# Products without a reader on TensorE's waits: a mixture-of-experts and windowed-attention kernel on one core

## The reference

```python
x = x + L0_ffn(L0_cond(x, cond_256, cond_64, ...))   # low-rank mixing, then 8 experts, the best 2 per token
x = x + L1_ffn(L1_cond(x, cond_256, ...))            # rotation by quaternions, then 2 layers

def L0_cond(x, spectral, rank, input_basis, mode_to_rank, output_basis):
    mtr = orthogonalize(mode_to_rank)                # Cholesky of a 64x64 Gram matrix, then its inverse
    proj = einsum('bsd,kd->bsk', x, input_basis) * spectral
    return (proj @ mtr * rank) @ output_basis

def layer(x):                                        # x: 8 x 512 x 256, heads of 64, windows of 128
    q, k, v = split(shift(x) @ wqkv); q, k = rotary(l2norm(q), l2norm(k))
    x = x + local_attention(q, k, v) @ wo
    h = layernorm(shift(x)) @ w1 + b1                # mean, variance, then gate and value halves
    a, g = split(h)
    return x + (a * gelu(g)) @ w2 + b2
```

## Time and profile before

| | us |
|---|---|
| median of 3 runs | 1883.55 (1882.44 to 1883.98) |
| the profiled execution | 1891.32 |
| its span, first to last instruction | 1889.6 |
| TensorE busy with products | 1724.4 (91%) |
| VectorE busy | 1081.8 (57%) |
| ScalarE busy | 915.0 (48%) |
| mean granted clock of TensorE | 0.96 of full speed |

### The profile page before, as it was taken

How to read it: one execution, slowest core, us unless ns; L and a number is a source line. 1 busy time by engine, 2 the same in 40 slices (tenths; PEclk the granted TensorE clock), 3 DMA queues, 4 the chain that set the end, 5 groups by cost and what they waited for, 6 DMA issues and landing times.

```text
span 1889.6 us, 28122 instructions
## 1 busy us (share of the span) xinstructions
PE 1724.4 (91%) x8535; PEld 1013.8 (54%) x8537; DVE 1081.8 (57%) x2991; ACT 915.0 (48%) x2195; POOL 170.8 (9%) x281
## 2 busy tenths in 40 slices
PE   5869997789999999999999999999999999999987
PEld 2547886455554555545555555455555555555555
DVE  7753332466575556565665665556656655565652
ACT  2203332355555646455646464556464646464741
POOL 5023331210020002000200020002000000000000
PEclk8759999789999999999999999999999999999998
DMA  8714442210010011000100110001001000000000
GB/s 238 275 33 120 121 120 78 70 34 12 1 34 1 1 34 34 23 13 1 35 1 1 34 34 23 13 1 35 1 1 34 12 23 1 1 1 1 1 23 11
DMA packets 59107, 72.31 MB, mean 38 GB/s; under 512 B 16644, under 2 KB 44888, under 8 KB 58840
## 3 DMA queue, kind: packets, MB, share of 16 engines
q1 hardware_dynamic: 50088, 58.77, 9.5%
q0 software_dynamic: 5376, 10.76, 2.3%
q10 hardware_dynamic: 3504, 1.06, 0.2%
HBM read 50.64 MB, written 19.92 MB: 37 GB/s over the span
## 4 chain that ended last, share of the span: by engine, by line
PE 68%; DVE 7%; issue 6%; ACT 1%; another core or an unknown queue 0%; DMA 0%; DVEq 0%; POOL 0%; ACTq 0%; POOLq 0%
PE pj L1444 16%; PE pj L1532 16%; PE pj L1538 7%; PE pj L1510 6%; PE sc L1467 6%; PE ob L1493 4%; PE pt L1478 3%; PE pj L1452 2%; PE pj L1434 1%; DVE pT L1346 1%; PE pj L1502 1%; DVE swapped L1721 1%; PE pj L1516 1%; PE pj L1544 1%; PE pj L1520 1%
## 5 line engine op out<-in xcount | busy, mean ns | idle before, releaser
L1444 PE MATMUL pj<-wqkv,xT 128*128 128x512 f32 x768 | 349.3, 605 | 6.4 <-issue 6.4
L1532 PE MATMUL pj<-xsq,w 128*128 128x512 f32 (+3 forms) x748 | 321.0, 579 | 6.5 <-DVE hid L1811 4.5
L1613 ACT ACTIVATE prob<-prob,nm 128x256 f32<-128x256 f32 (+1 forms) x512 | 239.8, 469 | 122.8 <-DVE nm L1750 118.0
L1750 DVE CUSTOM_DVE_ANT_0 prob<-sc,mask 128x256 f32<-128x256 f32 (+1 forms) x512 | 170.0, 386 | 132.4 <-issue 132.4
L1444 PEld LDWEIGHTS pj<-wqkv,xT 128*128 128x128 f32 x768 | 145.5, 193 | 184.7 <-issue 183.0
L1532 PEld LDWEIGHTS pj<-xsq,w 128*128 128x128 f32 (+1 forms) x748 | 137.3, 191 | 151.5 <-issue 145.3
L1716 DVE TENSOR_TENSOR direct<-qkraw,tabs 128x1024 f32<-128x1024 f32 x64 | 78.4, 1226 | 134.6 <-ACT qkraw L1584 134.6
L1478 PEld LDWEIGHTS pt<-ident,prob 128*128 128x128 f32 x896 | 105.0, 141 | 91.6 <-issue 65.3
L1478 PE MATMUL pt<-ident,prob 128*128 128x128 f32 x896 | 127.3, 276 | 23.8 <-DVE pT L1346 18.5
L1159 PE MATMUL yb<-w2m,hT 128*128 x576 | 136.3, 391 | 10.3 <-issue 8.5
L1467 PE MATMUL sc<-kT,qT 64*128 64x256 f32 (+1 forms) x1024 | 132.3, 377 | 14.1 <-DVE nm L1750 14.1
(11 more groups left out here) (306 smaller groups left out, 2254.9 us busy)
## 6 DMA issues: line engine op xcount, KB each, us to landing
w1x<-w_folded SPq DMA_DIRECT2D x72, 128.0 KB
slots_y<-yt SPq DMA_DIRECT2D x36, 256.0 KB
x1tok<-in_x_dram SPq DMA_DIRECT2D x10, 512.0 KB, 4.4
w1m<-in_L_ffn_w_dram SPq DMA_DIRECT2D x8, 512.0 KB, 5.6
w2m<-in_L_ffn_w_dram SPq DMA_DIRECT2D x8, 512.0 KB, 9.1
x_after_moe<-x1tok SPq DMA_DIRECT2D x8, 512.0 KB
x1out<-x_after_moe SPq DMA_DIRECT2D x8, 512.0 KB
out_dram<-x1out SPq DMA_DIRECT2D x7, 512.0 KB, 2.9
```

The lines of the kernel that those rows point to most:

```text
L1444: mm = pe.matmul(o[:, :], xs(s, c, w * P, P), wqkv[:, l, c, k * INNER:(k + 1) * INNER], start=(c == 0), stop=(c == DC - 1))
L1532: mm = pe.matmul(o[0:P if j == NJ - 1 else HJ[j], 0:tn], cols, h[:, c, t0:t1], start=(c == 0), stop=(c == DC - 1))
L1613: ins = a.activation(prob[:, g % 4, hh, 0:n], prob[:, g % 4, hh, 0:n], ACT.Exp, bias=nm[:, g % 4, hh:hh + 1], scale=-1.0, accum_out=rs[:, ...
L1750: ins = v.tensor_tensor_reduce(prob[:, g % 4, hh, 0:n], sc[par][:, hh, 0:n], mask[:, w % 2, 0:n], -1.0, 3.0e38, ALU.add, ALU.min, nm[:, g ...
```

## The change

TensorE gets further products whose results nobody reads. They are float32, 128x128 by 128x512, and each overwrites the same bank. In the routing there are 11 behind the router product, 1 behind L757, 6 behind L761 and 2 behind L764, each group ahead of the wait that follows. In the layers there are 12 behind the wait for `edge`, and in the second half of the last feed-forward 4 ahead of the wait of `mean`, 7 ahead of that of `var` and 7 ahead of that of the first `gate`. No wait, buffer or other instruction is changed.

```diff
                     router_product()
+                    def idle_products(count):
+                        for _ in range(count):
+                            pe.matmul(xb[:, 3, :], ident[:, :], projT_all, start=True, stop=True)
+                    projT_all = projT[:, 0, 0:512]
+                    idle_products(11)
                     pe.wait_ge(v_prep, AT_3)
                     pe.matmul(rk[lo, K + 3 * Q:K + 4 * Q], EHQ[hi, :], elim[hi, 1, :], start=True, stop=True
                               ).then_inc(quad_full, 1)
+                    idle_products(1)
                     pe.wait_ge(UT_copied, 1)
                     pe.wait_ge(w1p_copied, E)
                     pe.matmul(pb[0:K, 0:K], UT[:, :], rawT[:, :], start=True, stop=True).then_inc(mtr_full, 1)
+                    idle_products(6)
                     pe.wait_ge(z_ready, 1)
                     ...
                     mm.then_inc(m_full, 1)
+                    idle_products(2)
                     pe.wait_ge(m_ready, 1)
...
+                    def idle_products(count):
+                        for _ in range(count):
+                            pe.matmul(ob[:, :, :].rearrange("p c r -> p (c r)"), ident[:, :], rot[:, :, :].rearrange("p c d -> p (c d)"),
+                                      start=True, stop=True)
                     pe.wait_ge(edge, 1)
+                    idle_products(12)
...
                         elif kind == "mean":
+                            if t0 > 0:
+                                idle_products(4)
                             pe.wait_ge(xsum_ready, at(st["ffn"], i, FFN, 1, 1))
                             ...
                         elif kind == "var":
+                            if t0 > 0:
+                                idle_products(7)
                             pe.wait_ge(var_in, at(st["ffn"], i, FFN, 1, 1))
                             ...
                         elif kind in ("gate", "value"):
                             j = st["j"]
+                            if t0 > 0 and kind == "gate" and j == 0:
+                                idle_products(7)
                             pe.wait_ge(h_ready, at(st["ffn"], i, FFN, DC, DC))
```

## The result

The changed kernel takes **1908.24 us** (median of 4 runs, 1901.69 to 1910.95) against 1883.19 for the kernel before beside it: a ratio of 1.0125, 95% interval 1.0104 to 1.0146, so 20 to 27 us slower. The forecast was 1899, range 1891 to 1909: the sign is right, the time lies at the range's upper end, and some 9 us were not foreseen.

What follows compares the result with a forecast made beforehand. TensorE's chain (68% of the span) was taken as the bound, with waits and half clock behind them. Routing +7.3, lead +1, last half feed-forward +6.9 sum to +15.2 on 1883.55: 1899 us, range 1891 to 1909.

Steps and rivals of the forecast that it cites:

- The price of a product: All three places: a float32 product is two records, 0.86 us at 2.4 GHz and 1.71 us at 1.2 GHz.
- the bound of 3.6: TensorE's clock: from dense work to full clock takes 5 us, with 3.6 and 6 as bounds.
- The routing's terms: Routing, 20 products: the groups' overruns less the time given back by the clock, +7.3 us, bounds +6.0 and +11.4.
- from M's start to the hot products: Routing: the 64 records of L774 take 3.5 to 4 us at full clock instead of about 7.1, giving back 3.1.
- the second rival: Routing: its delay is hidden if the experts start on something other than the index; 7.3 falls away, 1891.5 us; 6%.
- The tail's terms: Last half feed-forward: +2.2, +3.7, +3.3 in the waits, -3.05 at the gates, +0.8 behind; sum +6.9 us.
- the term of the Gelu wait: Tail, behind the gates: the clock may fall in the wait for Gelu, +1.6 us at most, taken as +0.8.
- The lead's size: Lead, 12 products: +1 us taken, between -3.3 and +6.5, with +2.9 at the end of the first QKV.
- ScalarE's unexplained wait: Lead: a remote wait of 3.85 us until 350.70; ending as before, it swallows the 2.9 us delay.
- the sum's last: Whole kernel: +15.2 us from the profiled execution carried over unchanged to the median, 1883.55 + 15.2 = 1898.8 us.
- The first rival: All three places: a product takes one pass, 0.22 us at full clock, no wait is overrun; 1873 us; 6%.
- The third rival: All three places: products do not lift the clock, 1.71 us each and nothing given back; near 1943 us; 4%.

Runs made afterwards that it cites:

- the run of this part alone: Only the routing's 20 float32 products kept, lead and tail as in the kernel before: 1890.48 us, ratio 1.0046 to the kernel before.
- the run of the tail alone: Only the 18 float32 products of the last half feed-forward kept, none in routing or lead: 1889.63 us, ratio 1.0050 to the kernel before.
- the bfloat16 routing alone: Kernel before with bfloat16 products in the routing only (11, 1, 6, 2): 1885.27 us against 1882.69, ratio 1.0010.
- the bfloat16 kernel: Changed kernel with the same numbers of products in the same places, but bfloat16 factors: 1880.65 us against 1882.93 for the kernel before, ratio 0.9991.
- 64 one-column products: Kernel before with 64 one-column products in the first sequence's wait, 128 more TensorE instructions ahead of the loop: 1888.98 us against 1882.93, ratio 1.0036.
- 128 one-column products: Kernel before with 128 one-column products in the first sequence's wait, 16 KB of added TensorE code ahead of the loop: 1885.63 us against 1882.69, ratio 1.0011.

## Why the prediction was right, and where it was short

**The price of a product was right.** Forecast 0.86 us, and 11.9, 12.8 and 6.4 us for the groups of 11, 12 and 7; the rows of after have 11.60, 12.27 and 6.17. The clock rose 3.9 us after the first, between the bound of 3.6 and the 5 that I took. (Two slips in the recorded text change nothing: the clock of the lead was back at 340.5, not 340.7, and the routing's lower bound adds up to +6.3, not +6.0.)

**The routing's terms were right one by one.** L757 later behind the router product by 6.9 (forecast 7.2); the one product +0.6 (0.5), the six +2.5 (2.5), the two +0.3 (0.2); from M's start to the hot products -3.3 (-3.1). Sum +6.9 against +7.3, and +8.7 (5.3 to 11.9) in the run of this part alone. The hot products are unchanged, 17.03 us, and the second rival is out: from the first of them to the last expert product it is 216.05 us after and 216.27 before, so the experts moved along.

**The tail's terms were right.** +2.2, +3.7 and +3.3 in the three waits and -3.05 at the gates came out as 2.17, 3.71, 3.29 and -3.05; the term of the Gelu wait, 0.8 between 0 and 1.6, was 1.4. Sum +7.5 against +6.9. That term is the clock's and changes with the execution: the whole tail is +6.1 in the run of the tail alone, where the clock held, and +9.1 in the changed kernel's second trace, above the bound.

**The lead's size was right by luck, its reason was not.** From the last expert product to the second QKV after takes 35.06 us, 1.2 more than the run with the tail's products alone; but the four traces without products in the lead have 33.8 to 36.7 there, and the three with the twelve 34.2 to 36.0, so +1 is neither shown nor refuted. I let ScalarE's unexplained wait of 3.85 us decide the term. The same copy of the third window, in the traces of the tail alone, of the bfloat16 routing alone and of after:

```profile
346.94 0.37 ACT L1599 COPY xT<-pj 128x256 f32<-128x256 f32 x1 [2.12 <-PE pj L1437]
...
348.80 0.37 ACT L1598 COPY xT<-pj 128x256 f32<-128x256 f32 x1 [3.77 <-remote]
...
356.95 0.38 ACT L1599 COPY xT<-pj 128x256 f32<-128x256 f32 x1 [1.25 <-PE pj L1444]
```

The long wait comes in two of the four traces without products in the lead, and not in after, where the copy waits for TensorE alone and the rotations run at full clock. What ends it in those two stays unknown.

**The step that failed is the sum's last:** "That execution lies 7.8 above the median of the runs; the change is carried over as it is". Against the run with the tail's products alone, the profiled execution of before has 2.8 us more in the lead (that wait), 2.2 at the second jump (the clock falls behind it), 1.6 in the Gelu wait of the first half, where the clock fell, and 1.0 from the fold to the last expert product: 7.6 us that this other execution does not have. And **a term was missing**: the jumps, 3.1 + 3.2 us in after, which the prediction put at nothing without looking at them. That the time still lies in the range is luck so far: its top was made of the clock's and the lead's bounds, not of this. The account against the median is 6.9 + 1.2 + 7.5 + 6.3 = 21.9 us, of the 20 to 27 measured; the 2 or 3 left are within the interval. In the comparison of the two traces the missing 6.3 and that surplus cancel (the clock fell in the first half's Gelu wait of after too, so 6.0 of the 7.6 count; 21.9 - 6.0 = 15.9), and the sum of 15.2 seems confirmed by 16.7. Only the median showed that something was left out.

The first rival, cheap products, was built by the bfloat16 kernel: -10.6 was my price for it, it measured -1.7 (-4.3 to +1.1). Its trace shows that the clock, lifted in the routing's waits, did not last through the step behind (0.64, then 0.50), and that it fell at both jumps; how much of the missing 9 us these make in the median is not shown. The third rival is out by the stretches: 1.00 at 77.

What stays open: the first sequence's QKV of the other windows, from the second window's to the second sequence's first, takes 63.8 us in the profiled execution of after and 56.8 in the next one of the same kernel, with the clock going up and down there; no run tells what decides it. Of the 13 profiled executions four have 57 us there and nine 60 to 64, so it is as large as the effects sought here, and two traces can be compared only with it taken out (after and the run with the tail alone both have 63.8). The routing's own count could still be fitted; that wasn't tried in float32.

## What to carry to other kernels

Work without a reader is not free on an engine that works in order: fill a wait with less than it has, and price a group by the row of its own form and type, since in the routing and the tail here what overran went to the path in full (10.3 and 9.2 us) and the clock gave back only a third (3.3 and 3.05). Instructions added ahead of a loop move its start within the blocks of code, so look at the idle time at every jump back after such an edit, count the blocks of code that come there, and try another position before the edit itself is blamed. Compare a sum with the median and a second execution, not with one trace alone.

## What the runs showed that was not expected

- A jump back of TensorE costs 2.4 to 3.2 us of idle time in most positions, and 3.9 to 4.3 with 128 instructions added ahead of the loop; with 40 or 48 added, it stops a second time for 0.7 to 2.2 us.
- The clock falls at such a stop, and it can do so late: in after it is 1.00 through the 4.30 us of idle time at 812.2, then 0.50 for 3.4 us under dense work; with 64 one-column products it is 0.50 already from 799.8, within the idle time.
- Very short products can come in lots. Of the 128 one-column products the first 79 took 2.50 us; the other 49 came in small lots and needed over 9 us, which made the lead 6.5 us late. Timeline, 128 one-column products:

```profile
324.21 2.50 PE L1398 MATMUL ob<-ident_bf 128*32 128x1 bf16 x79 [3.77 <-POOL xT L1660]
327.13 0.30 PE L1398 MATMUL ob<-ident_bf 128*32 128x1 bf16 x6 [0.42 <-issue]
327.87 0.27 PE L1398 MATMUL ob<-ident_bf 128*32 128x1 bf16 x5 [0.43 <-issue]
...
336.47 0.48 PE L1398 MATMUL ob<-ident_bf 128*32 128x1 bf16 x12 [0.55 <-issue]
```

The lots are 0.72 us apart, or twice that, and nothing in the trace releases them. Late code would be a guess, and the transfers speak against it: one block comes at 326.47, in 1.41 us, and none between 327.9 and 336.5. The reason stays open.
